# Attention kernel: row maxima written straight into the query stack, and a denser first pass in three of four groups

## What is computed

```python
h = _layernorm(x) * (1 + ca) + sa
q, k, v = heads(Wq, bq), heads(Wk, bk), heads(Wv, bv)      # (8, 16, 1024, 16)
att = einsum('bhtd,bhsd->bhts', q, k) * scale              # causal mask, softmax over s
y = einsum('bhts,bhsd->bhtd', softmax(att), v)
x = x + ga * (y @ Wp + bp)
```

## Time and profile before

| | us |
|---|---|
| median of 3 runs | 5875.67 (5864.05 to 5878.0) |
| profiled execution | 5885.19, its span 5883.4 |
| attention stage in it | from about 30 to 2040, eight turns of 232 to 234 each after a lead-in |
| busy in the span | PE 4514.8 (77%), DVE 3568.6 (61%), ACT 2631.7 (45%), POOL 1731.0 (29%) |

### The profile page before, as it was taken

The page is one execution under the profiler, slowest core; times in us unless marked ns, Lnnn a source line. Parts: engine busy times, 40 slices in busy tenths (PEclk is TensorE's granted clock), DMA queues, the critical chain, the costliest instruction groups (busy, mean ns, idle before and its releaser), DMA issues. The chain is left out here.

```text
span 5883.4 us, 97285 instructions
## 1 busy us (share of the span) xinstructions
PE 4514.8 (77%) x31439; PEld 3167.8 (54%) x31439; DVE 3568.6 (61%) x8906; ACT 2631.7 (45%) x5436; POOL 1731.0 (29%) x1344
## 2 busy tenths in 40 slices
PE   3778777777787577887877887857788787887886
PEld 1333433333333266666666666646666666666665
DVE  3666666656666565665755755736565575575664
ACT  1434334334343254554544544535454454454543
POOL 1010110101101133433433433424343443343443
PEclk6889898989898789999988989979899898898988
DMA  4132242242222500000000000010000000000000
GB/s 93 41 79 44 57 99 45 57 73 62 65 54 55 109 15 14 13 11 15 12 13 15 10 13 17 10 55 14 20 16 15 20 15 20 20 14 18 16 15 21
DMA packets 177374, 202.00 MB, mean 34 GB/s; under 512 B 32479, under 2 KB 131259, under 8 KB 176707
## 3 DMA queue, kind: packets, MB, share of 16 engines
q1 hardware_dynamic: 176806, 194.81, 14.2%
HBM read 123.12 MB, written 63.25 MB: 32 GB/s over the span
## 5 line engine op out<-in xcount | busy, mean ns | idle before, releaser
L858 DVE TENSOR_REDUCE a_mx<-a_unit 128x1 f32<-128x512 f32 (+3 forms) x1584 | 817.6, 553 | 434.6 <-PE a_unit L677 303.9
L582 ACT ACTIVATE a_e_t<-a_ring 128x1024 f32<-128x1024 f32 (+3 forms) x768 | 615.4, 810 | 957.6 <-PE a_ring L702 735.8
L1367 POOL TENSOR_TENSOR b_e<-b_e,b_share 128x512 f32<-128x512 f32 (+1 forms) x512 | 527.5, 1030 | 1293.7 <-DVE b_share L1795 1293.7
L1470 ACT ACTIVATE b_e<-b_e,b_bias 128x256 f32<-128x256 f32 (+1 forms) x1024 | 498.6, 488 | 615.1 <-DVE b_bias L1775 614.0
L673 PE MATMUL a_unit<-a_k_st,a_q_st 96*128 96x512 bf16 (+3 forms) x1584 | 535.0, 345 | 206.9 <-DVE a_mx L858 167.6
L699 PE MATMUL a_ring<-a_q_st,a_k_st 99*128 99x512 bf16 (+3 forms) x1536 | 529.4, 358 | 167.0 <-DMA a_q_st<-maxima 89.9
L1573 PE MATMUL b_bank_m<-b_h_t_hi,b_w_hi 128*128 128x256 f32 x1584 | 476.0, 301 | 94.0 <-POOL b_h_t_lo L1373 71.9
L1573 PE MATMUL b_bank_p<-b_wqkv_hi,b_turned_hi 128*128 128x512 f32 x768 | 373.6, 486 | 182.5 <-ACT b_qk L1442 140.1
L673 PEld LDWEIGHTS a_unit<-a_k_st,a_q_st 96*128 96x128 bf16 x1584 | 154.4, 100 | 598.3 <-DVE a_mx L858 473.5
L1573 PE MATMUL b_bank_m<-b_h_t_lo,b_w_hi 128*128 128x256 f32 x1584 | 461.3, 291 | 0.0
L1573 PE MATMUL b_bank_m<-b_h_t_hi,b_w_lo 128*128 128x256 f32 x1584 | 460.6, 291 | 0.0
(11 more groups left out here) (217 smaller groups left out, 11767.5 us busy)
## 6 DMA issues: line engine op xcount, KB each, us to landing
a_q_st<-parts_q SPq DMA_DIRECT2D x216, 128.0 KB, 7.3
a_k_st<-parts_k SPq DMA_DIRECT2D x216, 128.0 KB, 9.7
b_fl<-f_rows SPq DMA_DIRECT2D x72, 256.0 KB, 4.0
parts_q<-a_qk_part SPq DMA_DIRECT2D x18, 768.0 KB, 3.5
parts_k<-a_qk_part SPq DMA_DIRECT2D x18, 768.0 KB, 3.8
a_xl<-in_L_attn_x SPq DMA_DIRECT2D x9, 1024.0 KB, 8.9
f_rows<-b_fr SPq DMA_DIRECT2D x33, 256.0 KB, 2.1
b_x_l<-x_rows SPq DMA_DIRECT2D x33, 256.0 KB, 3.1
```

Of the source, the lines that this page charges most:

```text
L582: act.activation(e_t[:, step % 2, 2 * pair:2 * pair + 2, 0:cols], slot[:, :].rearrange("p (h t) -> p h t", h=2)[:, :, 0:cols], ACT.Exp).th ...
L858: dve.reduce_max(mx[:, h, col:col + 1], slot[:, 0:cols], AX.X).then_inc(read.sem, 1)
L1367: pool.tensor_tensor(weights, weights, share[:, pp, :].unsqueeze(2) .broadcast_to([P, 2, 2 * WIN - lo]), ALU.mult).then_inc(e_done.sem, 1)
L1470: ins = act.activation(weights, weights, ACT.Exp, scale=-1.0, bias=bias[:, pp, hh:hh + 1], accum_out=total[:, pp, hh:hh + 1])
```

## The change

It has two parts. The first writes the three parts of the maxima from `m_part` into the rows of `q_st` with three transfers, one for a row, and drops the store into DRAM, the wait for it and the load. The semaphore `max_stored` goes; DVE, which waited for it before it overwrote `m_part`, waits for the previous group's three transfers. The second part changes the schedule of the first pass of groups 1, 2 and 3: it starts in step 0 of the group before, with six units a step, so that it ends with step 7, and the maxima are worked out in step 8. The first pass of group 0 stays as it is (start in step 3, six a step, maxima in step 11).

```diff
-PASS1_AT = {1: (2, 5, 11), 2: (0, 4, 11), 3: (0, 5, 10), 0: (3, 6, 11)}
+PASS1_AT = {1: (0, 6, 8), 2: (0, 6, 8), 3: (0, 6, 8), 0: (3, 6, 11)}
...
-        max_stored = [sig(f"a_max_stored{g}", 1, 16) for g in range(G1)]
-        max_loaded = [sig(f"a_max_loaded{g}", 1, 16) for g in range(G1)]
+        max_loaded = [sig(f"a_max_loaded{g}", MROWS - KROWS, 16) for g in range(G1)]
...
             def pass_maxima(g, i):
                 sp.wait_ge(max_split[g].sem, max_split[g].at(i, 1))
-                sp.dma_start(max_dram[g].rearrange("j (r t) -> r j t", t=P), m_part[:, :, :])\
-                  .then_inc(max_stored[g].sem, 16)
-                sp.wait_ge(max_stored[g].sem, max_stored[g].at(i, 1))
-                sp.dma_start(q_st[KROWS:MROWS, 4 * g:4 * g + 4, :],
-                             max_dram[g].rearrange("j (h t) -> j h t", t=T)).then_inc(max_loaded[g].sem, 16)
+                for j in range(MROWS - KROWS):
+                    sp.dma_start(q_st[KROWS + j:KROWS + j + 1, 4 * g:4 * g + 4, :]
+                                 .rearrange("j h (r t) -> j (h r) t", t=P), m_part[:, j, :])\
+                      .then_inc(max_loaded[g].sem, 16)
...
-            sp.wait_ge(max_loaded[0].sem, max_loaded[0].at(turns, 1))
+            sp.wait_ge(max_loaded[0].sem, max_loaded[0].at(turns, MROWS - KROWS))
...
-                    pe.wait_ge(max_loaded[g].sem, max_loaded[g].at(i, 1))
+                    pe.wait_ge(max_loaded[g].sem, max_loaded[g].at(i, MROWS - KROWS))
...
                     if not lead:
-                        stored = max_stored[(g - 1) % G1]
-                        dve.wait_ge(stored.sem, stored.at(i, 1))
+                        loaded = max_loaded[(g - 1) % G1]
+                        dve.wait_ge(loaded.sem, loaded.at(i, MROWS - KROWS))
```

## The result

The changed kernel took 5891.86 us (median of 9 runs, 5879.16 to 5901.55), the kernel before 5878.0 (9 runs beside it, 5864.05 to 5884.54). The ratio is 1.0023, with a 95% interval of 1.0014 to 1.0033. So it is slightly slower, by 0.14 to 0.33%, where the forecast had it 0.25% faster. The time is inside the range, and it is nearest to the price of rival B.

What follows compares the result with a forecast made beforehand. PE was taken to lead, with two waits for the maxima's transfer at group joins. Gains of 1.9 us a turn over eight turns (15) plus 1.4 in the lead-in, with 2 us allowed for turn 0, gave 5861 us; range 5824 to 5898.

Steps and rivals of the forecast that it cites:

- rival B: Groups 0 to 2: PE waits in dense steps and falls to 1.2 GHz; 2.5 us a turn, 5896 us; chance 0.18.
- group 1: POOL becomes late; transposes of x start 45.7 us after group 1's first values, against 39.9 before.
- From the normalisation to the transposes: End of group 1: POOL modulates x only after the last normalisation, 9.2 us before the transposes can begin.
- The transposes' clock: Transposes of x: after PE's idle time they run at 1.2 GHz, 3.50 us for 1.96, a loss of 1.5.
- Group 0: First values of group 1 come at 43.7 us instead of 51.8, both waits and low clock gone; gain 8.1 us.
- The direct write: Maxima into the query stack: one transfer and the wait between removed; landing taken as 2.0 us, bounds 1.4 and 5.
- The lead-in: Ahead of the loop, where the wait for the maxima is also open: the direct write gains 1.4 us once.
- Rival C: Direct write lands in 5 us behind the loads; group 3 starts 3 us later a turn, 5885 us; chance 0.10.
- Group 2: Maxima queue behind the next turn's loads; group 3 starts 0.3 us sooner, plus 0.8 from a shorter low clock.
- Group 3 and the tail: Last group of the turn and the tail behind it: claimed unchanged.
- Rival A: Group 1: DVE's gaps take up its own work and POOL is in time; 48 us gained, 5827 us; chance 0.22.
- The signs: Changed profile: PE waits 2 to 4 us for POOL; x transposes take 3.5; group 1 has no maxima wait, group 3 2-3.

Runs made afterwards that it cites:

- the run with other forms: The changed kernel with the maxima's copy and pairwise minimum on DVE made reductions and the remainder kept in PSUM: 5885.7 us, ratio 1.0022 to the kernel before.

## Why the prediction was wrong

**Wrong step: group 1.** Its mechanism was right in direction: at six units a step POOL is late and the transposes of x come later. What failed is the step from the last normalisation to the transposes, which let POOL and DVE work side by side, and the price of the pace, which had no term for the low clock. The sum set the transposes 45.7 us after the first values; they came 50.18 after in the mean. Four items lead from the forecast's loss of 5.8 + 1.5 = 7.3 us up to the second group's values to the measured 11.05 - 0.71 = 10.3:

- The baseline. The 39.9 us were read in the second turn. The mean of eight is 39.13: three turns showed 38.0, the other five 39.6 to 39.9. +0.8.
- The last normalisation. Forecast 33.2 + 3.3 = 36.5. It is exact where the granted clock was 1.00 (36.55), and 37.94 in the mean. +1.4. This is rival B's low clock in dense steps; the sum had no term for it. The evidence against B, group 3 at this pace with the clock high, did not carry over to a group where DVE has other work.
- From the normalisation to the transposes. Forecast 9.2, POOL's two instructions. Measured 12.2 (50.18 - 37.94): POOL's instructions held the copy and the cast, PE stood 4.47 us in step 8, still had three steps of scores to do when it went on, and in the second turn reached the transposes 3.7 us after POOL's end. +3.0. The forecast named POOL and DVE as neighbours and asked only which ends last, not whether they can work at once.
- The transposes' clock. Forecast 1.5 us at 1.2 GHz behind an idle PE. As PE came from scores, they took 1.96 us at the full level. -1.5, and the stretch behind them is 0.7 under before's for the same reason. Together -2.2.

0.8 + 1.4 + 3.0 - 2.2 = 3.0, and 7.3 + 3.0 = 10.3. The third and the fourth item are one event, and the run with other forms shows it: without the hold the third is gone (47.79 us to the transposes, of which the last normalisation takes 38.4), the loss of the fourth comes in, and the time is the same. So the hold, which looks like the culprit in the trace, cost nothing that the runs can tell. What the change lost it lost by the pace in group 1, which with POOL's chain behind it costs 11.5 us a turn against four units a step.

**Group 0: right.** Forecast 8.1 us, measured 7.70. Both waits and the low clock behind them are gone. Its explanation holds as well: with the maxima in step 10 the transfer is exposed again, though only 0.9 us of the gain went with it.

**The direct write: mis-sized.** Forecast 2.0 us to the landing in place of the old pair's 1.4 + 2.2, so some 1.6 less at an exposed join. It is 0.5 to 0.7 on an idle queue. The bounds of 1.4 and 5 us for the landing held (3.1), but the value taken was too low: an issue of a row costs 0.6 us on SP and not 0.3, and three stand in a line. In the sum it did little harm, since group 1's join was hidden anyway. The lead-in gained 0.3 us (a wait of 4.85 for 5.11), not 1.4. Rival C's sign, over 3 us on an idle queue, was just met (3.05 to 3.08 from DVE's last cast); its price, a later group 3, did not come to pass.

**Group 2: right, in part by luck.** Forecast -1.1, measured -1.19. PE waited for the maxima in seven turns, 1.1 to 5.3 us, as the forecast's signs said (2 to 3). Group 3 starts 28.2 us after the first load in the mean (forecast 27.9; before 30.0, which the forecast read as 29.8), and the loads start 1.1 us later after group 2's first values (forecast 1.6). The loads were the limit as claimed; the run with dense units and the loads behind the maxima shows that. But the write behind them took 4.3 to 8.5 us from DVE's cast to PE, not 2.0, and the maxima came earlier to make up for it.

**Group 3 and the tail: right**, -0.18.

**Rival A** asked whether DVE's own work hides in its gaps and POOL is in time. It does not: PE's own arrival without POOL is 43.8, and even that is 5.8 us over the 38.0 of four a step.

**The signs.** There is no wait for maxima at group 1, as said, and seven steps of it take 33.2 us at the full clock and up to 36.2 (forecast 33). But PE never waits for POOL, and the transposes take 1.96 us. By the forecast's list that pointed to rival A, and it misled: POOL was done before PE asked only because PE had been held itself. Rival B's sign, a granted clock under 0.85 in groups 0 and 1, was not met either (0.86 to 1.00 in the 36 us of group 1), though its mechanism was at work. That the time lies inside the stated range is no success of the sum; the range took in rival B's price, and slower had a chance of 0.18.

## What to carry to other kernels

When work is moved between engines' steps, the pace should follow from which engine bounds each stretch. DVE had 5 us of other work in group 1, and pressing its units into eight steps of twelve made PE wait first and DVE idle afterwards, while in group 0, where what waited behind the last step was the transfer, the same setting paid 7.7 us. A change that sets three values by one rule is better made one value at a time: group 1's was worth 1.1% (0.9968 to 0.9858) and group 2's cost 1.5% (0.9871 to 1.0023). And before a small copy or cast from SBUF to SBUF on VectorE is moved beside a long GpSimd instruction, look whether a reduction or an input in PSUM can do the same; but ask first what stands behind it, since here the stall was in front of a limit of the same length.

## What the runs showed of the hardware

- A VectorE copy of 128x16 from SBUF to SBUF (0.175 us alone) takes as long as the GpSimd instruction that it meets: 4.48, 1.24 and 0.70 us beside instructions of 4.50, 1.26 and 0.72. A cast from SBUF (0.21) took 3.34. A cast or a subtraction with PSUM as input (0.28) and a reduction (0.17) took their usual time in the same place.
- A transfer from SBUF into one partition in pieces of 256 bytes, 8 KB in all, landed 1.8 us after its issue in the median, and the issue kept SP for 0.6 us. What cost time was three issues in a line: issuing each part when it was made took 0.5 to 0.8 us off. No run here varied the size of the pieces.
- In a stretch in which PE and DVE wait for each other, a low TensorE clock delays DVE too: the same step took 5.39 us with a granted clock of 1.00 and 6.27 to 6.48 with 0.73 to 0.78, for 4.4 us of work on DVE each time.
- A wait moved to a later step of a program need not move the work: DVE, with nothing queued before it, took the maxima at the same moment in step 11 as in step 8.
